# Late expert tiles listed by rank and then by expert, and sums loaded at scatter counts that VectorE computes, in a decoder layer with eight experts

## What is computed

```python
gate_probs = jax.nn.softmax(jnp.einsum('bsd,de->bse', x, Wg) + bg, axis=-1)
topk_probs, topk_idx = jax.lax.top_k(gate_probs, TOP_K)          # TOP_K = 2, 8 experts
topk_probs = topk_probs / jnp.sum(topk_probs, axis=-1, keepdims=True)
...
h = jax.nn.gelu(jnp.einsum('bsd,edf->bsef', x, W1) + b1, approximate=False)   # 1024 wide
y = jnp.einsum('bsef,efd->bsed', h, W2) + b2
x = _layernorm(x + jnp.einsum('bsed,bse->bsd', y, weights), axis=-1)
```

## Time and profile before

| | us |
|---|---|
| median of 3 runs | 696.76 (696.32 to 698.15) |
| the profiled execution | 694.99 |
| its span, first to last instruction | 692.5 |

### The profile page before, as it was taken

How to read it: one execution, slowest core, us unless ns; L and a number is a source line. 1 busy time by engine, 2 the same in 40 slices (tenths; PEclk the granted TensorE clock), 3 DMA queues, 4 the chain that set the end, 5 groups by cost and what they waited for, 6 DMA issues and landing times.

```text
span 692.5 us, 22288 instructions
## 1 busy us (share of the span) xinstructions
PE 604.8 (87%) x8063; PEld 445.7 (64%) x8063; DVE 516.3 (75%) x1105; ACT 398.3 (58%) x846; POOL 291.1 (42%) x245
## 2 busy tenths in 40 slices
PE   2589889999999999989897887899999999999940
PEld 1357656666667766757564555777888888878820
DVE  5886898898775978767777997677766667666735
ACT  4334677857567477567868776355444444444414
POOL 4777583633454733443102011143444444444322
PEclk9879999999999999999999899799999999999995
DMA  8534343060331212313426016212333222233226
GB/s 275 163 102 121 111 136 126 14 172 2 85 103 55 66 36 77 98 59 86 137 87 198 2 32 210 73 32 36 52 53 50 48 48 47 48 48 53 42 46 219
DMA packets 39860, 59.75 MB, mean 86 GB/s; under 512 B 6768, under 2 KB 27504, under 8 KB 39632
## 3 DMA queue, kind: packets, MB, share of 16 engines
q1 hardware_dynamic: 32272, 48.12, 23.0%
q0 software_dynamic: 7488, 10.23, 9.1%
HBM read 34.08 MB, written 11.67 MB: 66 GB/s over the span
## 4 chain that ended last, share of the span: by engine, by line
PE 44%; DVE 9%; ACT 4%; issue 2%; DMA 2%; SPq 1%; ACTq 0%; POOL 0%; DVEq 0%
PE bank L1682 9%; PE bank L1684 5%; DVE mxc L1082 3%; PE scores L1672 3%; PE scores L1674 3%; PE scores L1673 3%; PE bank L1672 2%; PE bank L1674 2%; PE bank L1286 2%; PE bank L1673 2%; PE bank L1312 2%; ACT probs L742 2%; PE scores L1337 1%; PE scores L1409 1%; DMA w_sb<-acc_rows 1%
## 5 line engine op out<-in xcount | busy, mean ns | idle before, releaser
L742 ACT ACTIVATE probs<-scores 128x768 f32<-128x768 f32 (+1 forms) x128 | 114.5, 918 | 53.8 <-PE scores L1343 42.5
L627 POOL DMA_INDIRECT acc_rows<-x,slot_row x39 | 62.7, 1609 | 118.1 <-DVE x L1195 118.1
L1682 PE MATMUL bank<-w_sb,wp 128*128 x312 | 109.7, 379 | 1.8 <-DVE wp L1182 1.8
L1082 DVE TENSOR_REDUCE mxc<-scores 128x4 f32<-128x1024 f32 x64 | 76.5, 1218 | 20.3 <-PE scores L1357 20.0
L1684 PE MATMUL bank<-w_sb,wp 128*128 x312 | 85.1, 273 | 0.0
L813 ACT ACTIVATE probs<-scores,b_sb 128x128 f32<-128x128 f32 x160 | 45.6, 369 | 59.8 <-PE scores L1674 59.8
L813 ACT ACTIVATE probs<-bank,b_sb 128x128 f32<-128x128 f32 x152 | 43.6, 370 | 57.1 <-PE bank L1674 57.0
L1180 DVE CAST wp<-probs 128x512 f16<-128x512 f32 x78 | 34.7, 445 | 55.5 <-ACT probs L813 55.3
L1047 DVE TENSOR_REDUCE mx<-scores 128x6 f32<-128x768 f32 x64 | 60.0, 951 | 15.5 <-PE scores L1325 15.1
L1672 PE MATMUL scores<-xT,w_sb 128*128 128x128 f16 x320 | 60.9, 223 | 2.2 <-DVE xT L906 1.2
L589 POOL TENSOR_TENSOR w_sb<-w_sb 128x512 f16<-128x512 f32 x32 | 37.4, 1177 | 58.1 <-ACT w_sb L715 57.9
(11 more groups left out here) (264 smaller groups left out, 1717.7 us busy)
## 6 DMA issues: line engine op xcount, KB each, us to landing
w_sb<-w_sb SPq DMA_DIRECT2D x192, 64.0 KB, 2.3
wstage<-in_w_exp SPq DMA_DIRECT2D x16, 512.0 KB
w_sb<-in_w_exp SPq DMA_DIRECT2D x8, 512.0 KB, 5.1
wp<-in_w_exp SPq DMA_DIRECT2D x8, 512.0 KB, 3.9
x_sb<-in_x_by_feature SPq DMA_DIRECT2D x8, 256.0 KB, 3.4
ctx_raw<-in_ctx SPq DMA_DIRECT2D x8, 256.0 KB, 3.3
x_res<-in_x SPq DMA_DIRECT2D x8, 256.0 KB, 3.1
x_rows<-x SPq DMA_DIRECT2D x8, 256.0 KB, 3.1
```

What stands on the lines that cost most here:

```text
L627: nc.gpsimd.indirect_dma_start(out=acc_rows[:, :], out_offset=bass.IndirectOffsetOnAxis(ap=slot_row[:, n:n + 1], axis=0), in_=yb[n % 2], i ...
L742: nc.scalar.activation(probs[:, 2 * (k % 4):2 * (k % 4) + 2, 0:cols], ps_p[pair[u, k, b]][:, :, 0:cols], ACT.Exp, scale=(SELF_SCALE, CROSS ...
L1082: nc.vector.tensor_reduce(mxc[:, 2 * k:2 * k + 2, :], ps_p[pair[u, k, b]][:, :, :].rearrange("p h (a k) -> p h a k", a=2), axis=AX.X, op=A ...
L1682: mm(o[:, 0:2 * D], ah[:, u, f, :], weights(e, at, 2 * D), start=(f == 0), stop=(f == FC - 1), skip_group_check=True)
```

## The change

- The late places (11 to 38) are listed by rank first: the third tile of every expert, then the fourth of every expert, and so on. `gate_late_tiles` is rewritten in three parts: parts 0 and 1, eleven instructions on DVE, in the place of sixteen at n == 4, and part 2, eight instructions at n == 8. The expert of each late tile now comes from PE: a third product in `gate_table` (the choice of tiles by the lane's expert number), which DVE copies to `tile_e` in `gate_late_rows`. The unfilled places name expert 0 in place of 7.
- Part 2 computes for four points of the token list (after 10, 12, 14 and 16 token tiles) how many scatters must have landed: the largest count that any expert has before that point, rounded up to tiles, is the rank up to which the list must be done. In `gate_slots` DVE keeps the counts that this needs in four copies.
- The groups of sums are six (2, 4, 4, 2, 2 and 2 token tiles). SP waits for the computed count (16 for each scatter) that belongs to the end of the group, which it reads into a register: groups 1 to 3 for the first, then one for each of the others. The group that crosses the middle is moved in two transfers, for loads and stores. `fin` moves out of the weights' tile into half of `probs` and into `swaps`, which the expert tiles don't use by then.
- POOL waits for the last scatter behind the inverse roots, and SP too waits for it at its very end.
- `last_shift` is one instruction.
- The table of constants has ten columns more.

```diff
-LAST = [(0, 2), (2, 6), (6, 10), (10, 14), (14, 16)]
+LAST = [(0, 2), (2, 6), (6, 10), (10, 12), (12, 14), (14, 16)]
+SEEN_BY = [10, 12, 14, 16]
...
@@ block.sync
-            sp.wait_ge(sc_st, 16 * N_TILES)
+            sp.wait_ge(v_need, 1)
             for k, (t0, t1) in enumerate(LAST):
-                sp.dma_start(fin[:, t0:t1, :], acc_st_rows[:, t0:t1, :]).then_inc(f_ld[k], 16)
+                if k == 0 or t1 > SEEN_BY[0]:
+                    i = [k for k, end in enumerate(SEEN_BY) if end >= t1][0]
+                    scatters = sp.value_load(scatters_needed[0:1, i:i + 1], min_val=16, max_val=16 * N_TILES)
+                    sp.wait_ge(sc_st, scatters)
+                for a0, a1 in by_half(t0, t1):
+                    sp.dma_start(fin_at(a0, a1), acc_st_rows[:, a0:a1, :]).then_inc(f_ld[k], 16)
...
+            sp.wait_ge(sc_st, 16 * N_TILES)
...
@@ block.gpsimd
-            pool.wait_ge(sc_st, 16 * N_TILES)
             for k, (t0, t1) in enumerate(LAST):
                 inverse_root(frs[:, t0:t1], v_varf, k + 1, p_rsf)
+            pool.wait_ge(sc_st, 16 * N_TILES)
...
@@ gate_slots
+                if g:
+                    for i, end in enumerate(SEEN_BY):
+                        nc.vector.tensor_copy(seen_counts[:, i, :], rank[:, end - t0, :] if end < t1 else ps_rank[g][:, P:P + E])
...
+            def gate_late_tiles(part):
+                if part == 0:
+                    dve.wait_ge(pe_w[1], B)
+                    count_tiles(count, tiles, ltmp)
+                    link(nc.vector.scalar_tensor_tensor(kept, tiles[:, :], tab[:, C_RP:C_RP + 1], early[:, :], ALU.min, ALU.max))
+                    link(nc.vector.scalar_tensor_tensor(upto, tiles[:, :], tab[:, C_RP1:C_RP1 + 1], early[:, :], ALU.min, ALU.max))
+                    link(nc.vector.tensor_tensor(upto, upto, kept, ALU.subtract))
+                elif part == 1:
...
+                else:
+                    link(nc.vector.tensor_reduce(needed[:, :], seen_counts, axis=AX.X, op=ALU.max))
+                    link(nc.vector.tensor_scalar(needed[:, :], needed[:, :], 1.0 / P, 0.5 - 0.5 / P, ALU.mult, ALU.add))
+                    link(nc.vector.tensor_scalar(needed[:, :], needed[:, :], 1.5 * 2.0 ** 23, None, ALU.add))
+                    link(nc.vector.tensor_scalar(needed[:, :], needed[:, :], -1.5 * 2.0 ** 23, None, ALU.add))
+                    link(nc.vector.tensor_tensor(rows, tiles[:, :].unsqueeze(1).broadcast_to([P, n, E]),
+                                                 needed[:, :].unsqueeze(2).broadcast_to([P, n, E]), ALU.min))
+                    link(nc.vector.tensor_tensor(rows, rows, early[:, :].unsqueeze(1).broadcast_to([P, n, E]), ALU.max))
+                    link(nc.vector.tensor_reduce(needed[:, :], rows, axis=AX.X, op=ALU.add))
+                    nc.vector.tensor_scalar(scatters_needed[:, :], needed[:, :], 16.0, None, ALU.mult).then_inc(v_need, 1)
...
@@ gate_late_rows
+                nc.vector.tensor_copy(tile_e[:, at], ps_fin[1][:, 2 * n:3 * n]).then_inc(v_te, 1)
...
                 elif n == 4:
-                    gate_late_tiles()
+                    gate_late_tiles(0)
+                    gate_late_tiles(1)
...
+                elif n == 8:
+                    gate_late_tiles(2)
...
@@ last_shift
-                link(nc.vector.tensor_tensor(fnb[:, at], fmv[:, at, 0], frs[:, at], ALU.mult))
-                nc.vector.tensor_scalar(fnb[:, at], fnb[:, at], -1.0, None, ALU.mult).then_inc(v_nb, 1)
+                nc.vector.scalar_tensor_tensor(fnb[:, at], fmv[:, at, 0], -1.0, frs[:, at], ALU.mult, ALU.mult).then_inc(v_nb, 1)
...
@@ gate_table
+                if g:
+                    last = mm(ps_fin[g][:, 2 * (i1 - i0):3 * (i1 - i0)], tab[:, C_EOF:C_EOF + 1].broadcast_to([P, P]), slot_t[2][:, i0:i1],
+                              start=True, stop=True)
```

More of the change, by code:

```diff
@@ L61 @@
 C_RP = C_E16 + E
-C_ALL = C_RP + 1
+C_RP1 = C_RP + 1
+C_EOF = C_RP1 + 1
+C_BEFORE = C_EOF + 1
+C_ALL = C_BEFORE + E
 M_QUERY = 0
@@ L344, in decoder_layer @@
         yb = [x1[:, i, :] for i in range(2)]
-        fin = w_sb[:, 0:NT * D * 2].bitcast(F32).rearrange("p (t d) -> p t d", d=D)
+        fin_parts = [probs[:, 4:8, :].rearrange("p a n -> p (a n)").rearrange("p (t d) -> p t d", d=D),
+                     swaps[:, :].rearrange("p (t d) -> p t d", d=D)]
+        fin = [fin_parts[t // (NT // 2)][:, t % (NT // 2), :] for t in range(NT)]
+        seen_counts = wide[:, 0:len(SEEN_BY) * E].rearrange("p (i e) -> p i e", e=E)
+        needed = sb("needed", [P, len(SEEN_BY)])
+        scatters_needed = sb("scatters_needed", [P, len(SEEN_BY)], I32)
         fsmall = x2T[:, :, :].rearrange("p c t -> p (c t)")
@@ L473, in piece, with by_half, fin_at @@
             return n, stage, (n // 2 + 1) * 16, e, j
+        def by_half(t0, t1):
+            middle = NT // 2
+            return [(t0, middle), (middle, t1)] if t0 < middle < t1 else [(t0, t1)]
+        def fin_at(t0, t1):
+            first = t0 // (NT // 2) * (NT // 2)
+            return fin_parts[t0 // (NT // 2)][:, t0 - first:t1 - first, :]
         block = stack.enter_context(nc.Block())
@@ L537, in _ @@
                     sp.wait_ge(v_f, 1)
-                sp.dma_start(out_rows[:, t0:t1, :], fin[:, t0:t1, :]).then_inc(f_st, 16)
-            sp.wait_ge(f_st, 16 * len(LAST))
+                for a0, a1 in by_half(t0, t1):
+                    sp.dma_start(out_rows[:, a0:a1, :], fin_at(a0, a1)).then_inc(f_st, 16)
+            sp.wait_ge(f_st, 16 * sum(len(by_half(t0, t1)) for t0, t1 in LAST))
+            sp.wait_ge(sc_st, 16 * N_TILES)
         @block.gpsimd
@@ L838, in _ @@
                 for t in range(t0, t1 - (k == len(LAST) - 1)):
-                    last = nc.scalar.activation(fin[:, t, :], fin[:, t, :], ACT.Identity, bias=fnb[:, t:t + 1], scale=frs[:, t:t + 1])
+                    last = nc.scalar.activation(fin[t], fin[t], ACT.Identity, bias=fnb[:, t:t + 1], scale=frs[:, t:t + 1])
                 last.then_inc(a_f, 1)
@@ L1239, in last_shift @@
                 at = slice(*LAST[k])
-                link(nc.vector.tensor_tensor(fnb[:, at], fmv[:, at, 0], frs[:, at], ALU.mult))
-                nc.vector.tensor_scalar(fnb[:, at], fnb[:, at], -1.0, None, ALU.mult).then_inc(v_nb, 1)
+                nc.vector.scalar_tensor_tensor(fnb[:, at], fmv[:, at, 0], -1.0, frs[:, at], ALU.mult, ALU.mult).then_inc(v_nb, 1)
             for k, (t0, t1) in enumerate(LAST):
-                dve.wait_ge(f_ld[k], 16)
+                dve.wait_ge(f_ld[k], 16 * len(by_half(t0, t1)))
                 for t in range(t0, t1):
-                    last = nc.vector.bn_stats(fst[:, t, :], fin[:, t, :])
+                    last = nc.vector.bn_stats(fst[:, t, :], fin[t])
                 link(last)
@@ L1774, in _table @@
     t[:, C_RP] = lane % NT
+    t[:, C_RP1] = lane % NT + 1
+    t[:, C_EOF] = lane // NT
+    t[:, C_BEFORE:C_BEFORE + E] = np.arange(E) < lane[:, None] // NT
     return t
```

29 lines of the change are left out of this document (15 added, 14 removed).

## The result

In the first measurement the changed kernel took 686.39 us (median of 4 runs, 685.66 to 689.40), the kernel before beside it 696.54: ratio 0.9859 (0.9824 to 0.9894). Measured again twice, each time beside the kernel before on one chip, it came out at 687.61 against 694.45 (0.9899, 0.9874 to 0.9923) and at 688.72 against 695.26 (0.9911, 0.9888 to 0.9935). Times are medians; the ratios, with their 95% intervals, rest on mean times and can differ a little from the ratio of the medians. Over all runs of this study the kernel before has a median of 695.2 us (49 runs, 691.1 to 699.5, standard deviation 1.7) and the changed one 688.0 (16 runs, 685.3 to 691.4). The change gains about 7.2 us, 1.0%. The forecast was a gain of 7.5 us and 689.3 us, with a range of 688.0 to 692.5 that the first measurement misses by 1.6 us.

The account below looks back on a forecast made before the run. PE paces the tiles; then a chain of last scatter, first load, statistics, ACT's run and store sets the end. Ending -8.4 and loop +0.9 give -7.5 us: 687.5, carried to the median 689.3 us, range 688.0 to 692.5.

Parts of the forecast that it names:

- The first root: Ending, POOL: first inverse root at 671.46 where DVE asks for it at 671.43, so just covered.
- ACT's run: Ending: ACT scales 13 token tiles from 673.79 for 6.75 us, to 680.54; store and end add 3.60.
- Copies: First tile, DVE: four copies from PSUM ahead of the rank arithmetic add 0.5 us, ends 0 and 0.8.
- third product: PE's slot table: two passes more cost about 0.3 us, ends 0 and 0.5.
- the eight instructions: Tile 9, DVE: low half of the next slots 1.1 us late, just covered; costs 0.1 us, ends 0 and 0.6.
- only groups 1 to 3 matter: Ending: if all three later groups of sums still waited for scatter 39, only 0.6 us would be lost.
- The first burst: Loads from 635.6: five transfers, 1.25 MB, 5.7 us; next scatter has 2 us of cover, cost taken as 0.
- Rival 1: Ending: counts do not let the loads go early, so nothing of the 7.15 us is saved; 698.3 us; chance 0.05.
- Rival 2: Late tiles: scatter-adds meet rows just written and land later; at 6.0 us a tile, 708 us; chance 0.03.
- Rival 3: Tile loop: thinner cover; copies 0.8, table 0.5, the eight 0.6, burst 2.0, together 3.9 us; 692.3 us; chance 0.10.
- Rival 4: Ending: last scatter's issue blocked while DVE gathers statistics; first root 2 us later; 691.3 us; chance 0.07.
- carried to the median: 689.3: Last step of the sum: forecast 687.5 for the profiled execution, 1.77 below the runs' median of 696.76, moved to 689.3.

Follow-up runs that it names:

- curve: Kernel with fixed counts, with 2 to 12 small chained DVE instructions added behind the weighting of eight late tiles; one execution, tiles 0.0 to 1.3 us longer.
- one_count: Kernel with fixed counts, but all six groups of sums wait for the same 36 scatters; ratio 0.9920 to the kernel before.
- late_loads: Changed kernel with all six groups of sums loaded only after scatter 39; ratio 0.9999 to the kernel before.
- fixed_counts: Changed kernel without the computation of the counts; SP waits for the constants 32, 35, 35 and 36 scatters; 686.12 us, ratio 0.9884 to the kernel before.
- tab_only: Kernel before with ten more columns in its table of constants and nothing else; ratio 1.0013 to the kernel before.

## Why the prediction came out as it did

**The mechanism and the sum held.** The chain that I had read from the earlier trace rows was the one that ended last, and with the loads gone from its front DVE's statistics followed the last weighting at once. From the last weighting to the end of the span it was to be 15.9 us and was 15.7, with small errors both ways. The first root came 0.63 us after DVE asked for it (forecast 0.03), so that ACT's run began 0.26 us later than in my sum. The run took 6.49 us, not 6.75, and what follows it 3.3, not 3.6. That times counted from the start of the span agree still better (first statistics 668.25 expected, 668.07 measured; end of ACT's run 680.54 in both) is luck: attention ended 1.3 us earlier in this execution than in the profile before, and the loop took 1.2 us longer.

**The loop: 0.9 expected, 1.2 measured, with other shares.** Copies 0.3 for 0.5; third product 0.23 for 0.3; the eight instructions 0.7 for 0.1. These are one way to share it; without the counts the loop is as long as before, third product and all. The eight instructions are the term that failed in kind: I took PE's need for the low half from the start of the first matmul that reads it, and the curve shows that it is 0.8 us earlier. What the sum left out is the lead: 1.1 us of delay under 1.16 us of cover cost 0.7 us without a wait. My upper end for this term, 0.6, was just too low.

**The counts.** 32, 35, 35 and 36 were right: SP's loads stood at 636, 653 and 659. That only groups 1 to 3 matter was right for the statistics and missed what one_count showed: where the burst falls decides when the last scatters land, and POOL's roots hang on the last one. The first burst is four transfers, not the five of my sum (three into `probs`, one into `swaps`); its 1.25 MB were right. The forecast gave it 2 us of cover; in the changed kernel the scatter after it slipped by 0.9 us and no tile noticed.

**The rivals.** Rival 1 did not happen. Forced by late_loads, it gave 0.9999, so a change of nothing, where its sum had been 1.5 us over the kernel before (698.3 against 696.76); the interval, 0.9975 to 1.0023, holds both. Rival 2 did not happen: tiles late in the loop stand 5.5 us apart as before. Rival 3 happened in one of its four parts. Rival 4 did not happen as it was stated: scatter 39 was issued at 669.51 beside DVE's statistics in 1.55 us, as with DVE idle before. Its ground was weak already, for the scatters at 631.97 and 648.76 were issued beside DVE's work in 1.59 us, and only the first one had 1.89. What came late was scatter 38: its issue took 2.03 us in place of 1.55, scatter 39 was issued 0.5 us later for it, and DVE waited 0.63 us for the first root. The rule on the shared port pair (the Trainium skill, SBUF — State Buffer, "SBUF: two separate sides") would have POOL blocked while some DVE instructions run. The issue beside the statistics shows nothing of that, and scatter 38 can hardly be laid to it: DVE ended its last instruction beside that issue at 665.15 and stood idle for the rest, to 666.57. In the repeats that issue took 1.86 and 2.01; in fixed_counts, with DVE doing the same work at that place, it took 1.55, so no run here settles what decides it.

**What put the first result outside the range is the level and the spread, not the effect.** The step that failed is the last of the sum: "carried to the median: 689.3", on 696.76, the median of three runs, with 0.4 us allowed for scatter below. Over 49 runs the kernel before stands at 695.2 with a standard deviation of 1.7, so the level was 1.5 us too high; and the four runs of the first measurement, with a median of 686.4, lay 1.6 us below the 688.0 of all 16. The effect itself, 7.2 us for 7.5, took 0.2 back. Together that is the 2.9 us between 689.3 and 686.4. With the right level the same sum gives 695.2 - 7.5 = 687.7. The three runs shown had spanned 1.8 us, and the profiled execution, 1.8 below their median, was a fourth that said so. The near agreement of the effect is closer than the profiles can vouch for: by stages the ending gained 8.6 to 10.4 us, depending on which profile of before one takes, for the 8.4 of my sum, and the loop lost 1.2 for 0.9.

## What to carry to other kernels

When the first step of an ending is a reload of results that are nearly all final, ask of each part when its last writer is done: here a wait for the last of 39 scatters hid that the data had been ready after 36, and starting the loads early was worth some 9 us of ending for 1.2 us of loop. Put such a burst where the queue that it delays still has slack, not among its last entries. And when DVE work is slipped in front of something that PE waits for, don't count on its cover down to PE's first use: in this kernel the last 0.8 us of it were not free, and the tile paid before any wait showed. And a median of three runs is no level to hang a range of 4.5 us on when single runs spread by 8.

## What the runs showed of the hardware

- The expert tile's matmuls ran slower when the low half of their input came late but still before its first use: from 0.8 us ahead of use, each further 0.1 us of delay cost about 0.1 us of the tile (6 to 12 added instructions: 0.2 to 1.3 us). Only the tile with 12 shows a wait of PE, 0.48 us of the 1.3 that it lost.
- Seven loads of 2 MB issued within 3.5 us stretched a scatter-add of 128 rows from some 4.5 to 7.4 us between its issue and the next; four loads of 1.25 MB issued from 635.8 on delayed the scatter after it by 0.9 us. Without any load near, the same distance was 4.5 us in most profiles and 5.6 to 5.7 in two (late_loads, tab_only).
- The issue of a scatter on POOL took 1.59 us beside DVE's work in most tiles of the loop, 1.55 beside its statistics, and 1.84 to 2.06 in single tiles (the first three in every profile, scatter 38 or one near it in some), for a cause that stays open.
- Executions of one program differed by up to 8.4 us (691.1 to 699.5 for the kernel before), and 0.01 of mean granted clock goes with 4 to 5 us of it. Most of the spread stands in the stage up to the first rank arithmetic: it ended between 441.0 and 447.8 in the profiles of this study, of kernels that are the same up to there but for a few constants and copies, and in one stretch of it the clock was 0.94 to 1.00. The tile loop repeats within 0.1 us in two profiles each of the kernel before and of the changed one; a third of the changed one has 1.5 us more, in a first tile at a lower clock.
